# Second graph layer of a four-layer GNN: a quarter of the attribute adds moved from VectorE to GpSimd

## The reference

```python
src, dst = (edge_index[0], edge_index[1])
msg = jax.nn.relu(x[src] + edge_attr)
aggr = jax.ops.segment_sum(msg, dst, num_segments=N)
z = x + aggr
h = jax.nn.relu(z @ W1 + b1) @ W2 + b2
return _layernorm(x + jax.nn.relu(h), gamma, beta)
```

## Time and profile before

| what | us |
|---|---|
| median of three timed runs | 6502.33 |
| lowest and highest of them | 6499.54, 6507.79 |
| span of the profiled execution, first to last instruction | 6898.0 |
| gathers of the second layer, first to last start (profiled) | 1689.5 to 2858.3 |
| last accumulation of the second layer (profiled) | 2918.3 |

### The profile page before, as it was taken

How to read it: one execution, slowest core, us unless ns; L and a number is a source line. 1 busy time by engine, 2 the same in 40 slices (tenths; PEclk the granted TensorE clock), 3 DMA queues, 4 the chain that set the end, 5 groups by cost and what they waited for, 6 DMA issues and landing times. The chain is left out here.

```text
span 6898.0 us, 99476 instructions
## 1 busy us (share of the span) xinstructions
PE 4580.7 (66%) x17620; PEld 3435.1 (50%) x17621; DVE 4207.2 (61%) x10350; ACT 2924.2 (42%) x8245; POOL 4137.4 (60%) x3730
## 2 busy tenths in 40 slices
PE   7366666660455555586777777775567777777799
PEld 5234344430233333375666666664455555555688
DVE  4366666677455555684444444445589988988554
ACT  0133233335233333252222222222278988888543
POOL 1666666632666666326888888883367777777110
PEclk9566666675676766797766777777888988988899
DMA  6344444424555555316888888886556656666110
GB/s 202 106 109 110 110 109 109 110 75 153 161 180 176 173 172 176 119 63 119 132 131 131 132 131 131 132 131 183 178 161 187 187 177 185 188 180 185 41 33 28
DMA packets 704342, 947.56 MB, mean 137 GB/s; under 512 B 99439, under 2 KB 560847, under 8 KB 704176
## 3 DMA queue, kind: packets, MB, share of 16 engines
q0 software_dynamic: 277808, 587.53, 37.0%
q1 hardware_dynamic: 406928, 338.53, 17.1%
q10 hardware_dynamic: 19440, 19.79, 0.8%
HBM read 756.06 MB, written 189.40 MB: 137 GB/s over the span
## 5 line engine op out<-in xcount | busy, mean ns | idle before, releaser
L1712 POOL DMA_INDIRECT gcn<-c_update,c_target x832 | 1300.0, 1563 | 271.5 <-issue 231.9
L1308 PE MATMUL psum<-g_rows,g_onehot 128*128 x1664 | 635.5, 532 | 745.8 <-issue 240.9
L664 POOL DMA_INDIRECT e_rows<-hrow,e_idx x832 | 822.3, 988 | 463.2 <-issue 236.9
L2078 POOL DMA_INDIRECT s_rows<-kv,s_idx x832 | 798.3, 960 | 372.0 <-issue 224.5
L1200 POOL DMA_INDIRECT g_rows<-x,g_idx x784 | 765.2, 976 | 414.7 <-issue 222.2
L1308 PEld LDWEIGHTS psum<-g_rows,g_onehot 128*128 128x128 f32 x1664 | 396.7, 260 | 984.5 <-issue 928.2
L727 PE MATMUL psum<-e_rows,e_onehot 128*128 128x265 f32 x1664 | 668.9, 559 | 275.0 <-issue 112.2
L2181 PE MATMUL psum<-queries_sums,s_spread 128*128 x1664 | 518.3, 466 | 249.4 <-issue 148.4
L727 PEld LDWEIGHTS psum<-e_rows,e_onehot 128*128 128x128 f32 x1664 | 403.6, 266 | 478.4 <-DVE acc L821 191.3
L1276 DVE TENSOR_TENSOR acc<-acc,psum 128x256 f32 x832 | 349.4, 420 | 439.6 <-issue 189.1
L1664 PE MATMUL psum<-support,c_mix 128*128 x1664 | 610.1, 531 | 0.0
(11 more groups left out here) (360 smaller groups left out, 9315.4 us busy)
## 6 DMA issues: line engine op xcount, KB each, us to landing
g_attr<-in_edge_attr SPq DMA_DIRECT2D x196, 512.0 KB
c_srow<-rows_src SPq DMA_DIRECT2D x208, 256.0 KB
e_drow<-rows_dloc SPq DMA_DIRECT2D x208, 128.0 KB
c_feat<-in_edge_feat SPq DMA_DIRECT2D x832, 32.0 KB
s_drow<-rows_dloc SPq DMA_DIRECT2D x208, 128.0 KB
n_sums<-gcn SPq DMA_DIRECT2D x100, 256.0 KB
e_rows<-hrow,e_idx POOLq DMA_INDIRECT x832
edge_rows<-c_edge_rows SPq DMA_DIRECT2D x208, 64.0 KB
```

What stands on the lines that cost most here:

```text
L664: pool.indirect_dma_start(rows[u][:, s, 0:D + H], None, k.hrow, bass.IndirectOffsetOnAxis(ap=idx[u][:, s:s + 1], axis=0)).then_inc(gathere ...
L1308: pe.matmul(k.psum[:, s, 0:D], onehot[q % 2][:, s, :], rows[:, bass.ds(m[q % 2 * GROUP + s], 1), :].rearrange("p o d -> p (o d)"), start=T ...
L1712: pool.indirect_dma_start(k.gcn[a], bass.IndirectOffsetOnAxis(ap=target[q][:, a:a + 1], axis=0), update[q][:, a, :], None, compute_op=ALU. ...
L2078: pool.indirect_dma_start(rows[at.u][:, st, 0:2 * D], None, k.kv, bass.IndirectOffsetOnAxis(ap=idx[at.u][:, st:st + 1], axis=0)).then_inc( ...
```

## The change

GpSimd adds the attributes to the fourth tile of each group itself, straight from the buffer `g_attr` in SBUF, between its groups of gathers: after the gathers of group n it adds for group n-2 (`PAUSE = 2`). VectorE's add and ScalarE's copy to PSUM shrink from four tiles to three. SyncE's load now also waits until GpSimd has used the old buffer, and ScalarE's relu also waits for GpSimd's add.

```diff
+    SHARE, PAUSE = GROUP - 1, 2
...
+        last_added = sem("g_last_added")
...
+        def shared_tiles(at):
+            return rows[:, bass.ds(at.slot, SHARE), :].rearrange("p s d -> p (s d)")
+
+        def moved_attr(at):
+            return flat(k.psum[:, 4 + 2 * (at.q % 2):6 + 2 * (at.q % 2), :])[:, 0:SHARE * D]
...
                 wait_if_any(sp, moved, g - BATCH + 1)
+                wait_if_any(sp, last_added, g - BATCH + 1)
...
+            def add_last(t, n):
+                n, r = n % (2 * ROUND), t * 2 + n // ROUND
+                pool.wait_ge(gathered[n % ROUND], (r + 1) * (16 * GROUP))
+                pool.wait_ge(attr_landed[n % BATCH], (r * 2 + n % ROUND // BATCH + 1) * 16)
+                to = rows[:, n * GROUP + SHARE, :]
+                pool.tensor_tensor(to, to, attr[n % BATCH][:, SHARE, :], ALU.add).then_inc(last_added, 1)
+
             for t in ends_apart(pool, 10):
                 for n in range(2 * ROUND):
                     if not isinstance(t, int) or t * (2 * ROUND) + n < TILE_GROUPS:
                         gather(t, n)
+                    at = n - PAUSE
+                    if not isinstance(t, int) or 0 <= t * (2 * ROUND) + at < TILE_GROUPS:
+                        add_last(t, at)
...
-                act.copy(flat(k.psum[:, 4 + 2 * (at.q % 2):6 + 2 * (at.q % 2), :]), flat(attr[at.q % BATCH][:])
-                         ).then_inc(moved, 1)
+                act.copy(moved_attr(at), flat(attr[at.q % BATCH][:, 0:SHARE, :])).then_inc(moved, 1)
...
                 act.wait_ge(added, at.g + 1 + 2)
+                act.wait_ge(last_added, at.g + 1)
...
-                dve.tensor_tensor(tiles_of(at), flat(k.psum[:, 4 + 2 * (at.q % 2):6 + 2 * (at.q % 2), :]),
-                                  tiles_of(at), ALU.add).then_inc(added, 1)
+                dve.tensor_tensor(shared_tiles(at), moved_attr(at), shared_tiles(at), ALU.add).then_inc(added, 1)
```

## The result

| kernel | median us | runs | lowest to highest |
|---|---|---|---|
| before | 6504.03 | 4 | 6499.54 to 6507.79 |
| changed | 6620.95 | 4 | 6616.02 to 6947.32 |

The changed kernel is slower by 116.9 us: the ratio is 1.0179, 95% interval 1.0163 to 1.0195. The execution of 6947.32 us was a disturbed one (its granted clock is 0.618 against 0.77 in the other three), and comparisons leave such executions out, here and in what follows.

What follows compares the result with a forecast made beforehand. The prediction took GpSimd's gathers to bound the second layer's edge phase in timed runs. Its terms, 94 + 11 + 5 = 110 us on 6502.3, gave 6612 us, 1.7% slower; its case's own range was 6590 to 6680, the 8-in-10 range from 6490.

Steps and rivals of the forecast that it cites:

- The phase is bound by GpSimd: Second layer's edge phase: in timed runs GpSimd's gathers run through at 5.04 us per group; chance 0.60.
- The reason given for it: Stalls on VectorE's sequencer belong to the recording; 388.0 us of waits account for the 395.7 us between span and median.
- VectorE's 52 us: VectorE's add, 1024 to 768 columns: saves 52 us of its time, worth 0 because GpSimd paces the phase.
- ScalarE's shorter copy: ScalarE's copy to PSUM, three tiles for four: worth 0, as the engine is busy 315 of 950 us.
- Rival A: Second layer's edge phase: stalls are real and VectorE bounds, so the change is faster, 6460 us; chance 0.16.
- GpSimd's add, 94 us: GpSimd's add between gathers: 0.62 us less 0.14 of covered idle, 0.48 per group, 94 us; ends 94 and 288.
- Meetings with the one-hot: GpSimd's add meets VectorE's one-hot over SBUF in 24% of groups, at half of 0.46 us: 11 us, ends 0 and 22.
- Waits: GpSimd's add waiting for its gathers and attributes, and SyncE's new wait for the add: all met, 0.
- rival C: Next gather restarts late after each GpSimd add: 6806 us in full, 6677 if a third do; chance 0.07.
- The end, 5 us: End of the layer: the relu waits for a later add, group 193 ready 7.7 us later; 5 us, ends 0 and 10.
- Rival B: Stalls are real and pace VectorE by instructions, not work: no change, 6500 us give or take 10; chance 0.17.
- The sign that the gap between profiled span and timed median would shrink by up to 100 us: Changed profile: if it still has stalls, their waits absorb the 94 us, so the gap shrinks by up to 100 us.

Runs made afterwards that it cites:

- e11: The changed kernel without GpSimd's add and the two waits on it, on a chip without stalls: 6480.44 us against 6494.18, ratio 0.9976.
- e12: The kernel before plus a GpSimd add per group for which nobody waits, on a chip without stalls: 6618.09 us against 6494.18, ratio 1.0189.
- e1: The kernel before, unchanged, profiled again on a chip with stalls: 6963.61 us, with the kernel before at 6956 us beside it.
- e13: The kernel before, unchanged, profiled again on another chip with stalls: 6960.53 us, beside 6964.32.
- e3: The kernel before plus a GpSimd add per group for which nobody waits, on a chip with stalls: 6933.07 us against 6955.98, ratio 0.9966.
- e2: The changed kernel without GpSimd's add and the two waits on it, on a chip with stalls: 6959.74 us against 6955.98, ratio 0.9991.
- e5: The changed kernel with VectorE's one-hot cut to one element per group: 6572.69 us, ratio 1.0112 to the kernel before.
- e6: The kernel before with VectorE's one-hot cut to one element per group: 6458.42 us, ratio 0.9930.
- e10: The changed kernel, no edit, on another chip without stalls: 6610.65 us against 6494.18 for the kernel before, ratio 1.0179.
- e9: The kernel before with the one-hot made of four 128x128 operations with one tensor input each: 6465.15 us against 6503.84, ratio 0.9944.
- e8: The changed kernel with GpSimd's add one group of gathers behind instead of two: 6627.42 us, ratio 1.0195 to the kernel before.
- e4: The changed kernel with two tiles of four on GpSimd instead of one, on a chip with stalls: 7014.63 us against 6955.98, ratio 1.0079.

## Why the prediction was right, and where it was not

**The phase is bound by GpSimd where the times were taken: right.** This was the choice on which all hung. e11 shows it directly: gathers at 5.18 us per group, VectorE waiting for them 169 times. The extra add of e12 shows it from the other side, since it costs the full amount with nobody waiting for it.

**The reason given for it: wrong.** The prediction took the stalls to belong to the recording, and cited a page on the block that writes trace records. On the chips of e1 and e13 the timed runs are as long as the profiled span, and both have the stalls. The 395.7 us between span and median are, as far as the record shows, the difference between two chips. The step "if they belong to the recording" failed. The account behind it (388.0 us of waits in two phases against 395.7 to be explained) pointed at the right place: without stalls, in e11, the first layer's gathers take 1070.1 us instead of 1284.4 and the second's 1015.7 instead of 1168.8, 367 of the 420 us between the two spans. So the conclusion held although its reason did not: that the timed runs lack the stalls follows from the gap between span and median, whatever makes the stalls. It holds for chips like the one that gave the times, and that the timed runs fell on one is luck as far as the forecast goes. On a chip with stalls e3's extra add cost nothing, and whether the changed kernel is slower there is open.

**VectorE's 52 us and ScalarE's shorter copy, worth 0: nearly.** e11 is 0.24% faster than the kernel before, about 14 us. Rival A, under which VectorE's 52 us count in full, is out on both kinds of chip, since e2 and e11 save 0 and 14.

**GpSimd's add, 94 us: the mechanism right, the term mis-sized.** The price was taken from a row of 623 ns; the adds here take 737 undisturbed. The operation of that row reads its second input as few values, each repeated along the columns (line 2449), and this add reads two full inputs; whether that makes the 0.11 us was not tested. Its cover was right: a gather's idle time falls from 0.30 to 0.16 us around an add. Gather to gather across an add is 1.86 us, not the 1.7 forecast. Measured by e5 and e6 it is 0.58 us per group, 113 us.

**Meetings with the one-hot: the frequency right, the size too low, and one side missing.** 43 of the adds in the changed kernel's trace take over 1 us, near the 24% of groups forecast, but these lose some 0.5 us each, not half of 0.46. In e10 the adds take 860 ns in the mean against 735 in e5, 24 us in all, where 11 were forecast. The missing side is the gathers: e11's take 1015.7 - 989.2 = 26.5 us more than e6's, with no add anywhere. That loss was in the kernel before already, and it is the kind of loss that e9 takes back. There it may be larger: against the kernel before itself e6 gains 45 us (interval 28 to 64) and e9 39 us (26 to 47). About the lock, the Trainium skill, "SBUF — State Buffer", section "SBUF: two separate sides", names VectorE operations with two SBUF inputs among those that exclude a GpSimd one. The runs agree: with one tensor input in e9 the gathers are no longer stretched. e9 alone could not show that the input matters, since it also cuts the one-hot into four short operations; but VectorE's add of 0.95 us, with one of its two inputs in PSUM, stretches neither the gathers of e11 that it overlaps (0.95 us) nor the adds of e5 (745 ns at most).

**Waits, and start and end:** the add never waited in the phase (1.3 us in all, once, at the end), which e8 confirms, and the next gather starts at most 0.17 us behind each add, so rival C is out. The end, 5 us, was near: from the last gather's start to the last accumulation it is 48.0 us in e10 and 44.5 in e11, so 3.5.

**Sum.** On the chip of e10 to e12 the add and its waits cost 130.2 us (e10 against e11), or 123.9 by the idle add (e12), where 94 + 11 + 5 were forecast. The shorter work on VectorE and ScalarE saves 13.7, where 0 was forecast. The difference, 116.5, is the change. These figures are differences of the same medians, so that they add up is no check of its own. How the 130 split is less certain: the gathers' stretches give 113 for the add with nothing to meet (e5 and e6) and, for meetings, 1147.0 - 1102.1 = 44.9 us from e5 to e10 less the 26.5 that were there before, so 18. By the times, which for e5 and e6 have intervals of 18 us to either side, the change costs 114.3 us without the one-hot (e5 against e6) and 116.5 to 116.9 with it. The second count puts next to nothing on meetings, because it starts from the kernel before, in which the one-hot already costs 45. The two counts differ by about the 14 us of the shorter add, and this suggests that these 14 are fewer meetings of one-hot and gathers; without a trace of the kernel before without stalls that is not shown. The forecast of 110 came out close because an add priced too low and a saving priced at 0 partly cancel.

**Rival B** described the chips with stalls rightly: there 52 us less work on VectorE changed nothing (e2), as if the stalls were a matter of how fast instructions follow each other. Its mark, that each slow instruction takes the same 691 to 700 ns, came from a stretch of four; over the whole phase of that trace they reach 1067 ns. e4 has no slow instruction in the phase in which the others wait for GpSimd. What makes a sequencer stall on some chips was not found.

**What the profile was to show:** the adds of VectorE (0.95 us) and the copies of ScalarE (0.79) came as forecast. The sign that the gap between profiled span and timed median would shrink by up to 100 us could not be read, since the two profiles differ in whether they have stalls.

## What to carry to other kernels

Compare the span of a profile with the timed median before reading a wait from it: if they differ by more than the runs scatter, trace and times may come from chips that behave differently (6898.0 against 6502.33 us here), and the bound in the trace need not be the bound in the time. Look at the sequencer's own instructions too; a register instruction that takes 0.7 us instead of 0.04 tells of a state and not of the kernel alone. Work moved to an engine that paces a phase costs nearly its full length (0.58 us of 0.74) however idle the engine looks (60% busy here), and work that keeps that engine from being held up pays even when it makes another engine busier.

## What was not expected of the hardware

- Two of four chips ran the kernel before in 6956 and 6964 us, the others in 6504 and 6494. In the profiles from the first two single register instructions of VectorE's sequencer take about 0.7 us in stretches; in the others the same instruction takes 40 ns. It is not VectorE alone: SyncE's register instructions beside the loads of attributes reach 727 ns in e1 and 65 in e10.
- The stretches were gone from the one phase in which the other engines waited for GpSimd throughout (e4, on a chip with stalls), while the first layer of the same execution had them.
- An indirect DMA issued by GpSimd is held up by a VectorE operation with two SBUF inputs too: 992 ns in the mean (e11) against 959 without it (e6), and 1.06 us for those that the operation overlaps.
- An add of two full inputs of 128 x 256 takes 737 ns on GpSimd, where a 128 x 256 operation in another phase took 623.
